# Places of the steps in the common order of all engines, set anew in every stage of a four-layer transformer kernel

## Chip, cores and metric

One core of a Trainium2 chip. The metric is the time of the device in microseconds (us), the median of several runs. The engines are named as in the profile: PE is TensorE (PEld its weight loads), DVE is VectorE, ACT is ScalarE, POOL is GpSimd and SP is SyncE, which here issues all DMAs.

## The reference

x has the shape (2, 1024, 256): two batches of 1024 tokens. Four layers run one after the other. Each has self-attention, cross-attention to a context of 77 tokens, and an MLP; each of the three parts is added to x and has a layer norm ahead of it whose scale and shift come from a conditioning vector. In short:

```python
for layer in (L0, L1, L2, L3):
    h = ada_ln(x, cond)                       # 16 heads
    q, k, v = heads(h @ Wq), heads(h @ Wk), heads(h @ Wv)
    x = x + softmax(q @ k.T * scale) @ v @ Wo + bo      # 1024 x 1024 scores a head
    h = ada_ln(x, cond)
    x = x + softmax(heads(h @ Wq2) @ heads(ctx @ Wk2).T * scale) @ heads(ctx @ Wv2) @ Wo2 + bo2
    h = ada_ln(x, cond)
    x = x + gelu(h @ W1 + b1) @ W2 + b2       # L3: a gated MLP of twice the width
```

Layers 0 and 1 have heads of width 16, layers 2 and 3 of width 64. Layer 2 also turns q and k by rotary position factors (rope), in both attentions. All of it is fp32.

## The kernel before

**Stages.** The work runs in stages: for each layer a self-attention, a cross-attention and an MLP stage. For layers 0 and 1 (narrow) self and cross are laid into one plan; for layers 2 and 3 (wide) each stage has its own. At the end of a plan all engines drain and wait for each other. In the profiled execution the stages lie about here: narrow self 75 to 575 us and 880 to 1375 us, narrow cross up to 745 and 1548, their MLPs behind them; layer 2: self 1697 to 2640, cross 2710 to 3003, MLP to 3175; layer 3: self 3175 to 4050, cross 4100 to 4385, MLP to 4535.

**Common order.** All engines walk one list of steps, `order`. A step such as ("cs", S, n, j) has a part for each engine that takes part in it: `tensor_program`, `scalar_program`, `vector_program`, `gpsimd_program` and `sync_program` each loop over the whole list and issue their own instructions of every step, with waits on semaphores for what the others must have done. So an engine never takes a step out of turn, and the order of the list is the order of every engine's queue. The list is made by `Plan`: `put` gives each step a place, a number counted in units of the stage (lo for one step, or spread evenly from lo to hi), and `close` sorts by place, with ties in order of entry.

**Units.** In a self stage a unit is a group of heads (4 narrow, 2 wide) times 512 queries, in 8 key tiles. Per tile and half: `score` (PE: K times Q into PSUM; ACT: exponential, L1469) and `av` (PE, L1194). Scores are shifted by each query's negated maximum, which the steps of the unit ahead make: `max` (PE scores the other way round, L1087 wide and L1091 narrow; DVE reduces, L1757 and L1761), narrow only `mjoin` (DVE joins two halves, in the tile NMX, L1776), `mturn` (PE transposes, L1151 or L1149; DVE copies, L1788; SP sends the row into the query tile by DMA, L2144). The output: `fin` (ACT copies, L1479), the sums of the exponentials, `norm`, `proj` (PE, L1236 wide and L1246 narrow; DVE adds to x, L1850 wide and L1854 narrow). Wide units sum the exponentials by `acc_p` (POOL, tiles 0 to 5, L2031 and L2035) and `acc_v` (DVE, tiles 6 and 7, L1814), then `sum` (PE, L1204) and `norm` in two halves (DVE: reciprocal L1829, product L1831). Narrow ones use `sums16` (PE L1213, DVE L1822), `spread16` (ACT, L1509) and `norm` (PE L1221, DVE L1838).

**Wide cross units** (32 a stage, 2 heads and 512 queries each): `cs` for each head (PE scores, L1015; DVE takes the maximum, L1797; ACT makes exponentials with their sums, L1490), `cnorm` (DVE: reciprocal, L1806; POOL: product, L2022), `cturn` (PE transposes, L1118; ACT copies, L1498), `cav` (PE, L1130), `fin` (ACT, L1479), `proj` (PE L1236, DVE L1850).

**Work beside the units.** `nat64`, `p16`, `val16` and `v64` make Q, K and V from the normed input (PE, with copies on ACT and differences on DVE, L1728 where there is no rope). With rope a chain follows each `nat64`: copy (ACT L1435), `rcos` (DVE L1742, POOL L2008), `rturn` (POOL L2015 and L2016), `rhigh` (ACT L1441), `rlow` (DVE L1749). `keep16`, `stack16`, `qstack` and `kstack` are DMAs on SP that lay Q and K out for the heads (stack16: L2127, 6 transfers a group in a cross stage). `w_load` and `w_split` bring weights, `m_load` (SP, L2278) and `m_split` (DVE L1929, POOL L2041) those of the MLP. `norm_put` places the layer norm of the next part: statistics, root, `ln_norm` (DVE L1649), `ln_turn` (PE L1036, ACT L1408), `ln_split` (DVE, up to L1662), `ln_bias`. In an MLP stage `up` (PE, ACT, DVE) and `down` (PE, L1324) alternate.

**PSUM.** The free banks are handed out in turn by `take`; a step that takes a bank waits until it was freed three takes before (wide self: two). `small` is another ring, of one bank, for `mturn` and `sum` in wide self stages.

The functions that set the places are `core64_steps` (L633), `core_steps` (L657), `kv64_steps` (L687) and the loop over the stages (L750 on). The two that decide what a unit looks like are short in their core:

```python
            for at, step in ((-1.25, ("cs", S, u.n, 0)), (-0.85, ("cs", S, u.n, 1)), (-0.45, ("cnorm", S, u.n)),
                             (0.2 * S.L.rope, ("cturn", S, u.n)), (0.5 + 0.2 * S.L.rope, ("cav", S, u.n)),
                             (0.51 + 0.2 * S.L.rope, ("fin", S, u.n)), (1.3 + 0.15 * S.L.rope, ("proj", S, u.n, 0))):
                plan.put(u.n + at, 0, [step])
```

## Time and profile before

| what | value |
|---|---|
| runs of the kernel before | 4522.99 us median of 3 (4517.64 to 4530.47) |
| profiled execution | 4537.6 us; its span, first to last instruction, 4535.8 us |
| mean granted clock of TensorE | 0.948 |
| PE, DVE, ACT, POOL busy | 90%, 66%, 46%, 30% of the span |
| DMA | 269.28 MB, mean 59 GB/s |

How to read it: a line such as "PE PS L1118 <- POOL t L2022: 33.7, 32, 3.5" says that PE, ahead of its instructions of line 1118, stood idle for 33.7 us in all, in 32 cases, at most 3.5 us, until GpSimd's instruction of line 2022 had ended. In a timeline the brackets hold the idle time ahead of an instruction and what ended it. The granted clock is 1 at 2.4 GHz and 0.5 at 1.2 GHz, so 0.948 is a mean over stretches at either.

### The profile page before, as it was taken

The numbers are of one execution on the slowest core, as the hardware profiler recorded it, in microseconds if no ns is written. First come the engines' busy times: TensorE is split into PE (matmuls) and PEld (weight loads), VectorE is DVE, ScalarE is ACT, GpSimd is POOL, SyncE is SP. The second block draws the span as 40 slices with busy tenths as digits, with TensorE's granted clock in tenths as the row PEclk, the third lists the DMA queues.
The fourth block names the chain that finished last, engine by engine and source line by source line (L and its number), as shares of the span: only waits on it lengthen the run. The fifth ranks groups of instructions, "written<-read, shape, count | busy, mean of one in ns | idle before, by whom it ended". The sixth has DMA issues, their size and how long they took to land.

```text
span 4535.8 us, 55477 instructions
## 1 busy us (share of the span) xinstructions
PE 4070.6 (90%) x20428; PEld 2486.0 (55%) x20428; DVE 3010.2 (66%) x4405; ACT 2076.4 (46%) x3756; POOL 1349.6 (30%) x664
## 2 busy tenths in 40 slices
PE   7999979799998888998999967888999999997889
PEld 5343357634335675555555545666555555546668
DVE  5888755688885666777777844345677777764355
ACT  2656645255564543443444435553444344435541
POOL 1100011100001035655555543321444444441120
PEclk8999989899998999999999978998999999998999
DMA  4223230312323142331333222323232222214220
GB/s 131 39 43 49 44 70 24 56 30 43 47 44 63 32 88 63 66 65 39 65 66 66 63 65 67 70 61 63 69 70 60 67 66 66 60 47 108 68 54 20
DMA packets 151983, 269.28 MB, mean 59 GB/s; under 512 B 34090, under 2 KB 67812, under 8 KB 150688
## 3 DMA queue, kind: packets, MB, share of 16 engines
q1 hardware_dynamic: 151712, 265.72, 27.9%
q8 instruction: 163, 2.67, 0.3%
q14 instruction: 108, 0.88, 0.1%
HBM read 105.01 MB, written 29.64 MB: 30 GB/s over the span
## 4 chain that ended last, share of the span: by engine, by line
PE 38%; DVE 8%; ACT 4%; POOL 4%; issue 4%; SPq 3%; DMA 1%; POOLq 0%; DVEq 0%; ACTq 0%
PE PS L1015 19%; PE PS L1194 7%; PE PS L1087 4%; PE PS L1236 4%; PE PS L1324 2%; DVE t L1757 2%; SPq L2173 2%; ACT t L1490 1%; DVE PS L1829 1%; SPq L2190 1%; POOL t L2035 1%; PE PS L1118 1%; POOL t L2022 1%; POOL t L2008 1%; PE PS L1204 1%
## 5 line engine op out<-in xcount | busy, mean ns | idle before, releaser
L1015 PE MATMUL PS<-t 128*128 128x512 f32 (+4 forms) x7896 | 1988.9, 384 | 160.4 <-ACT t L1469 24.8
L1469 ACT ACTIVATE t<-PS 128x512 f32<-128x512 f32 (+2 forms) x1600 | 1166.9, 750 | 1124.7 <-PE PS L1015 1118.3
L1015 PEld LDWEIGHTS PS<-t 128*128 128x128 f32 (+2 forms) x7896 | 1253.8, 188 | 708.9 <-issue 253.5
L1194 PE MATMUL PS<-t 128*32 128x512 f32 (+2 forms) x4352 | 809.7, 610 | 0.2
L1757 DVE TENSOR_REDUCE t<-PS 128x1 fp32r<-128x1024 f32 x512 | 622.0, 1220 | 281.4 <-PE PS L1087 275.8
L1761 DVE TENSOR_REDUCE t<-PS 128x1 f32<-128x512 f32 x1024 | 651.4, 684 | 73.1 <-PE PS L1091 70.7
L2035 POOL TENSOR_TENSOR t<-t 128x1024 f32<-128x1024 f32 x256 | 617.6, 2412 | 133.6 <-ACT t L1469 106.9
L1091 PE MATMUL PS<-t 96*128 96x512 bf16 x1024 | 370.3, 394 | 34.8 <-DVE t L1761 14.3
L1087 PE MATMUL PS<-t 128*128 128x512 f32 x1024 | 339.9, 415 | 58.8 <-DVE t L1757 36.4
L2031 POOL TENSOR_TENSOR t<-t 128x1024 f32<-128x1024 f32 x64 | 155.0, 2422 | 734.4 <-PE PS L1204 442.1
L1194 PEld LDWEIGHTS PS<-t 128*32 128x32 f32 (+2 forms) x4352 | 170.7, 122 | 329.1 <-issue 324.4
L1972 POOL TENSOR_TENSOR t<-t 128x2048 f32<-128x2048 f32 x24 | 112.0, 4668 | 788.1 <-DMA t<-in_rows 528.6
L1091 PEld LDWEIGHTS PS<-t 96*128 96x128 bf16 x1024 | 97.1, 98 | 358.2 <-DVE t L1761 135.4
L1236 PE MATMUL PS<-t 128*128 128x256 f32 x1024 | 260.3, 399 | 27.5 <-DVE t L1742 10.9
L1850 DVE TENSOR_TENSOR t<-PS,t 128x1024 f32<-128x1024 f32 x128 | 156.3, 1221 | 166.3 <-PE PS L1236 166.3
L1087 PEld LDWEIGHTS PS<-t 128*128 128x128 f32 x1024 | 195.5, 197 | 127.6 <-DVE t L1757 53.3
L1236 PEld LDWEIGHTS PS<-t 128*128 128x128 f32 x1024 | 197.7, 199 | 69.2 <-issue 23.9
L1829 DVE RECIPROCAL PS<-PS 128x256 f32<-128x256 f32 x128 | 224.7, 1755 | 11.8 <-PE PS L1204 11.8
L1324 PE MATMUL PS<-t 128*128 128x256 f32 x1536 | 219.0, 295 | 10.4 <-DVE t L1946 5.8
L1324 PEld LDWEIGHTS PS<-t 128*128 128x128 f32 x1536 | 207.6, 199 | 22.8 <-DVE t L1946 5.5
L1490 ACT ACTIVATE t<-PS,t 128x77 f32<-128x77 f32 x512 | 159.3, 325 | 132.3 <-DVE t L1797 132.1
L1946 DVE TENSOR_TENSOR t<-t 128x512 fp32r<-128x512 f32 x128 | 113.6, 888 | 138.8 <-ACT t L1572 137.5
(131 smaller groups left out, 3804.9 us busy)
## 6 DMA issues: line engine op xcount, KB each, us to landing
t<-t SPq DMA_DIRECT2D x640, 128.0 KB, 2.5
t<-scr_n SPq DMA_DIRECT2D x288, 128.0 KB, 6.4
t<-t SPq DMA_DIRECT2D x128, 256.0 KB, 3.8
scr_n<-t SPq DMA_DIRECT2D x72, 256.0 KB, 2.3
t<-t SPq DMA_DIRECT2D x256, 64.0 KB, 2.0
t<-in_L_Wg SPq DMA_DIRECT2D x16, 768.0 KB, 4.6
t<-in_L_W SPq DMA_DIRECT2D x36, 256.0 KB, 3.2
t<-in_L_Wo SPq DMA_DIRECT2D x64, 128.0 KB, 2.5
```

The costliest lines, as they stand in the source:

```text
L1015: ins = e.matmul(out, l, r, start=i == 0, stop=i == len(terms) - 1, tile_position=tp)
L1087: ins = e.matmul(o[:, 512 * h:512 * h + 512], u.smq[j][qt], u.smk[j][h], start=True, stop=True)
L1091: e.matmul(o, u.smq[j][qt], u.smk[j][half], start=True, stop=True).then_inc(*bank_full[k].inc(nth))
L1194: ins = e.matmul(banks[S.ot][wd * j:wd * j + wd, :], u.v[j][kt], P[0:S.pr, j, :], start=kt == 0, stop=kt == S.nkt - 1, tile_position=(0, w ...
L1236: ins = e.matmul(o[:, 256 * q:256 * q + 256], S.OR[n % 2][:, 128 * q:128 * q + 128], u.wo[:, :], start=True, stop=True)
L1324: ins = e.matmul(banks[4 + q][:, 0:D], l, r, start=m == 0 and t == 0, stop=m == 7 and t == 2)
L1469: e.activation(dst, src, ACT.Exp, scale=S.L.scale).then_inc(*expd.inc((S.i, i)))
L1490: ins = e.activation(S.PQ[n % 3][:, j, t, :], o[:, 256 * t + CT * b:256 * t + CT * b + CT], ACT.Exp, bias=S.NM[n % 3][:, at], accum_out=S. ...
L1757: e.tensor_reduce(S.MT[m % 2][:, S.nqt * j + qt:S.nqt * j + qt + 1], o, AX.X, ALU.max, negate=True).then_inc(*bank_free[k].nth(nth))
L1761: e.tensor_reduce(S.NMX[:, 4 * j + qt, half:half + 1], o, AX.X, ALU.max).then_inc(*bank_free[k].nth(nth))
L1829: e.reciprocal(o[:, hs], o[:, hs]).then_inc(*recip_made.inc((S.i, n, h)))
L2035: e.tensor_tensor(S.AP_[:, :, :], S.AP_[:, :, :], P[1][:, :, :], ALU.add).then_inc(*pool_summed.inc((S.i, n, kt)))
```

## The change

No step is added or removed. The numbers given to `put` change in every stage; so the common list, and with it the queue of every engine, has another order. Two places need more than a number. The narrow stages' NMX is held twice, by turns of the unit, because the first max steps of the next unit now stand ahead of the last transposition of this one; SBUF use stays as it was, by a smaller filler. And in layer 2 one group makes the second half of its queries ahead of the first, so the DMA that stacks them waits for both halves. The diff, cut to its core:

```diff
@@ attention_tiles
-            S.NMX = sbt(c, [128, 16, 2])
+            S.NMX = [sbt(c, [128, 16, 2]) for _ in range(2)]
@@ core64_steps
-            for at, step in ((-1.25, ("cs", S, u.n, 0)), (-0.85, ("cs", S, u.n, 1)), (-0.45, ("cnorm", S, u.n)),
-                             (0.2 * S.L.rope, ("cturn", S, u.n)), (0.5 + 0.2 * S.L.rope, ("cav", S, u.n)),
-                             (0.51 + 0.2 * S.L.rope, ("fin", S, u.n)), (1.3 + 0.15 * S.L.rope, ("proj", S, u.n, 0))):
+            places = ((-1.25, -0.774, -0.45, -0.038, 0.7, 0.71, 1.523) if S.L.rope else
+                      (-1.51, -1.07, -0.59, -0.071, 0.5, 0.56, 1.921))
+            for at, step in zip(places, (("cs", S, u.n, 0), ("cs", S, u.n, 1), ("cnorm", S, u.n), ("cturn", S, u.n),
+                                         ("cav", S, u.n), ("fin", S, u.n), ("proj", S, u.n, 0))):
...
-                    plan.put((i + 1.2) / k, 0, [("acc_p", S, n, kt)])
+                    plan.put((i + 0.489) / k, 0, [("acc_p", S, n, kt)])
...
-                    plan.put((i + 1.3) / k, 0, [("acc_v", S, n, kt)])
+                    plan.put((i + 0.859) / k, 0, [("acc_v", S, n, kt)])
...
-                    for at, step in ((2.76, ("sum", S, n)), (2.77, ("fin", S, n)), (4.2, ("norm", S, n, 0)),
-                                     (5.2, ("norm", S, n, 1)), (7.2, ("proj", S, n, 0))):
+                    for at, step in ((2.76, ("sum", S, n)), (2.77, ("fin", S, n)), (3.451, ("norm", S, n, 0)),
+                                     (4.2, ("norm", S, n, 1)), (7.2, ("proj", S, n, 0))):
@@ core_steps (sums16, spread16, norm, proj, proj)
-        tail = (0.2, 0.45, 0.7, 1.2, 1.45) if S.cross else (0.07, 0.25, 0.4, 0.53, 0.72)
+        tail = (0.2, 0.182, 0.7, 1.2, 1.45) if S.cross else (0.07, 0.082, 0.4, 0.53, 0.72)
@@ narrow cross
-                            at = (-3, 3.05)[b] + 0.8 * ch
+                            at = (-3, 3.132)[b] + 0.444 * ch
...
-                        plan.put((-1.95, -1.95, 0.05, 0.05, 4.5, 4.6, 6, 8)[g], 0, [("stack16", S, g)])
-                        plan.put((-1.2, -0.7)[g] if g < 2 else 2 * g - 2.2, (-0.7, -0.2)[g] if g < 2 else 2 * g - 0.7,
+                        plan.put((-1.95, -1.95, 0.05, 0.05, 4.5, 6.232, 6, 8.524)[g], 0, [("stack16", S, g)])
+                        plan.put((-1.306, -0.663)[g] if g < 2 else 2 * g - 1.981, (-0.7, 0.504)[g] if g < 2 else 2 * g - 0.7,
...
-                        plan.put(5 + 0.9 * j, 0, [("m_load", M, j)])
+                        plan.put(3.494 + 0.9 * j, 0, [("m_load", M, j)])
@@ narrow self
-                    plan.put(5.6, 7.6, [("val16", S, 1, t) for t in range(8)])
+                    plan.put(2.989, 7.245, [("val16", S, 1, t) for t in range(8)])
...
-                        plan.put(max(n - 1.3, 0), n - 0.3, max_steps(S, n))
+                        plan.put(max(n - 1.331, 0), n - 0.362, max_steps(S, n)[:-1])
+                        plan.put(n - 0.3, 0, max_steps(S, n)[-1:])
@@ wide cross (o = 4 * g - 9)
-                            nat64_chain(plan, S, g, 0, (o + 1.3, o + 2.9), (0, 0.15, 0.3, 0.95, 1.1))
+                            nat64_chain(plan, S, g, 0, (o + 1.647, o + 2.737), (0, 0.022, 0.3, 0.968, 1.081))
...
-                            plan.put(o + 2.3, o + 3.7, nat64_steps(S, g, 0))
+                            plan.put(o + 3.125, o + 3.7, nat64_steps(S, g, 0))
...
-                        plan.put(2 * pi - 4.5, 0, [("qstack", S, pi)])
+                        plan.put(2 * pi - 3.632, 0, [("qstack", S, pi)])
@@ wide self, rope (o = 4 * g - 4)
-                            plan.put(o + (0.1 if g != 4 else 0.45), o + (0.5 if g != 4 else 0.75),
+                            plan.put(o + (0.684 if g != 4 else 0.45), o + (0.5 if g != 4 else 1.194),
...
-                            for qk, at in ((1, (0.35 + late, 0.8 + late * 0.8)), (0, (1.25 + late * 0.5, 1.65 + late * 0.2))):
+                            for qk, at in ((1, (0.35, 0.81)), (0, (1.234, 1.65))) if g != 4 else (
+                                    (1, (0.65, 1.04)), (0, (2.114, 1.613))):
@@ wide self, no rope (v64, nat64 of K, nat64 of Q)
-                        for at, to, steps in zip((0.1, 0.55, 1.2) if g != 4 else (0.55, 1.0, 1.5),
-                                                 (0.5, 1.1, 1.9) if g != 4 else (0.95, 1.45, 1.95),
+                        for at, to, steps in zip((0.226, 0.856, 1.776) if g != 4 else (0.561, 1, 1.212),
+                                                 (0.5, -0.232, 1.9) if g != 4 else (0.95, 1.408, 1.988),
@@ MLP (layer norm of the next stage: first place, gap of the statistics, pace)
-                plan.put(max(2 * (i % 4) - 2.5, -2) if way == "up" else 2 * i + 0.2, 0, [("m_split", S, j)])
+                plan.put(max(2 * (i % 4) - 2.5, -2) if way == "up" else 2 * i + -0.122, 0, [("m_split", S, j)])
...
-                        plan.put(at + m + 2.5, 0, [("down", S, b, half, m)])
+                        plan.put(at + m + 2.696, 0, [("down", S, b, half, m)])
...
-                    at, gap, pace = (17.65, 0.05, 1.2) if b else (0.9, 0.35, 2)
+                    at, gap, pace = (17.808, 0.05, 0.913) if b else (0.9, 0.714, 2)
@@ vector_program
+                if m >= 2:
+                    w.wait_ge(max_part, (S.i, m - 2))
                 o, k, nth = full(w, ("max", S.i, m, j, qt, half))
-                e.tensor_reduce(S.NMX[:, 4 * j + qt, half:half + 1], o, AX.X, ALU.max).then_inc(*bank_free[k].nth(nth))
+                e.tensor_reduce(S.NMX[m % 2][:, 4 * j + qt, half:half + 1], o, AX.X, ALU.max).then_inc(*bank_free[k].nth(nth))
```

The rest of the diff moves further steps by less (places of the layer norms, of the key and value work of layers 2 and 3, of the first group's nat64 in the MLP stages).

## Rows read from the trace of the kernel before

**Rows 1.** The page: its head line and part 1 (busy time of each engine).

```profile
span 4535.8 us, 55477 instructions
PE 4070.6 (90%) x20428; PEld 2486.0 (55%) x20428; DVE 3010.2 (66%) x4405; ACT 2076.4 (46%) x3756; POOL 1349.6 (30%) x664
```

**Rows 2.** Busy time by stretch; columns in the first line, x counts instructions, PEclk mean granted clock.

```profile
core 0: us, PE busy (x) PEld busy (x) DVE busy (x) ACT busy (x) POOL busy (x), PEclk, DMA share, GB/s
...
1697.00:2640.00 943.00, 871.09 (x3666) 503.68 (x3666) 699.68 (x652) 395.70 (x634) 545.07 (x247) 0.97 0.28 60
2710.00:3003.00 293.00, 243.34 (x1276) 182.50 (x1275) 126.29 (x227) 163.35 (x589) 106.31 (x70) 0.91 0.27 62
3175.00:4050.00 875.00, 836.14 (x3604) 489.04 (x3605) 626.72 (x610) 366.11 (x600) 386.15 (x160) 0.99 0.28 64
4100.00:4385.00 285.00, 239.66 (x1304) 183.00 (x1304) 121.30 (x222) 156.67 (x594) 50.17 (x35) 0.94 0.31 72
```

**Rows 3.** Waits of PE in 4100:4385, layer 3's cross stage (total us, times, longest).

```profile
PE PS L1118 <- POOL t L2022: 33.7, 32, 3.5
```

**Rows 4.** Timeline of one unit of layer 3's cross stage (start us, duration us).

```profile
4255.45 1.23 DVE L1850 TENSOR_TENSOR t<-PS,t 128x1024 f32<-128x1024 f32 x1 [1.25 <-PE PS L1236]
...
4256.60 0.19 DVE L1806 RECIPROCAL t<-t 128x8 f32<-128x8 f32 x1
...
4256.87 1.22 POOL L2022 TENSOR_TENSOR t<-t 128x616 f32<-128x616 f32 x1 [5.29 <-DVE t L1806]
...
4258.14 1.10 PE L1118 MATMUL PS<-t 128*77 128x128 f32 x8 [0.56 <-POOL t L2022]
```

**Rows 5.** Waits of PE in 2710:3003, layer 2's cross stage.

```profile
PE PS L1130 <- ACT t L1498: 21.7, 13, 3.9
PE PS L1118 <- POOL t L2022: 12.0, 9, 6.6
PE PS L1236 <- ACT t L1490: 4.3, 10, 1.2
PE PS L1236 <- DVE t L1742: 4.2, 6, 1.0
```

**Rows 6.** Groups by line in 2710:3003: GpSimd's rope work (busy us, mean ns).

```profile
L2008 POOL TENSOR_TENSOR t<-t 128x1024 f32<-128x1024 f32 x12 | 28.3, 2359 | 74.6 <-ACT t L1435 57.2 <-issue 17.4
...
L2016 POOL TENSOR_TENSOR t<-t 128x512 f32<-128x512 f32 x12 | 15.2, 1269 | 0.0
```

**Rows 7.** Timelines of SP and PE in layer 0's cross stage; waits of PE in 1375:1548.

```profile
638.98 5.54 SPq L2127 DMA_DIRECT2D t<-scr_n  x12
...
645.33 0.55 SPq L2144 DMA_DIRECT2D t<-t  x1
...
656.98 1.07 PE L1015 MATMUL PS<-t 97*77 97x512 bf16 x2 [7.53 <-DMA t<-t]
...
PE PS L1015 <- DMA t<-t: 4.5, 1, 4.5
```

**Rows 8.** Waits of PE in 1697:2640, layer 2's self stage.

```profile
PE PS L1087 <- DVE t L1757: 18.7, 12, 5.2
...
PE PS L1204 <- DVE t L1814: 10.0, 8, 1.8
...
PE PS L1151 <- DVE t L1831: 2.7, 3, 1.5
```

**Rows 9.** Waits of PE in 880:1375, layer 1's self stage.

```profile
PE PS L1149 <- DVE t L1776: 4.0, 3, 2.3
```

**Rows 10.** The instructions of L1509 (spread16) in 75:575.

```profile
L1509 ACT ACTIVATE t<-t x15: 618/631/632, 151.4 to 569.7; 128x512 f32<-128x512 f32 x15
```

**Rows 11.** Waits of PE in 745:880, the end of layer 0's MLP.

```profile
PE PS L1015 <- DVE t L1662: 6.6, 1, 6.6
```

**Rows 12.** L1814 (acc_v) and L1749 (rlow) in 1697:2640: duration ns min/median/max.

```profile
L1814 DVE TENSOR_TENSOR t<-t x62: 1206/1218/3473, 1757.3 to 2626.4; 128x1024 f32<-128x1024 f32 x62
...
L1749 DVE TENSOR_TENSOR t<-t x28: 1207/1604/3409, 1750.1 to 2508.6; 128x1024 fp32r<-128x1024 f32 x28
```

54 lines of the change are left out of this document (27 added, 27 removed).

## Prediction

> **What bounds the kernel now.** I read the page first, then the busy time by stage, then in each attention stage what TensorE (PE) waited for, and last the timeline where one wait came back every unit. The page shows a PE kernel: 4070.6 us busy of a span of 4535.8 [rows 1]. No step is added or removed, so PE's own work stays as it is, and the change can only move the 465 us in which PE stood still and the time that a low clock added.
>
> By stage [rows 2] the self-attention of layers 2 and 3 is PE at 92% and 96% (871.09 of 943, 836.14 of 875), while the two wide cross-attention stages stand at 83% and 84% (243.34 of 293, 239.66 of 285), with a granted clock of 0.91 and 0.94 against 0.97 and 0.99. Per microsecond the cross stages have the most to give. In layer 3's, PE waits for GpSimd's cnorm multiply 32 times, once in every unit, 33.7 us in all [rows 3], 1.05 us each. The timeline of one unit says why [rows 4]: VectorE adds the projection (4255.45, 1.23 us), only then takes cnorm's reciprocal (4256.60), GpSimd multiplies (4256.87, 1.22 us), and PE starts cturn the moment that ends, after 0.56 us idle. The reciprocal was not late for want of data; it stood behind the add, which stood behind PE's projection. In layer 2's cross stage the same engine waits otherwise [rows 5]: 21.7 us for ScalarE's cturn copy ahead of cav, 12.0 for GpSimd, and 4.3 and 4.2 ahead of the projection, 42.2 in these four.
>
> **The change, part by part.** A place matters only where it puts a step past another step on the same engine. The orders below follow from the numbers of the diff, sorted for one engine at a time.
>
> (a) Cross, layer 3. PE's cycle was cturn(n), cs1(n+1), proj(n-1), cav(n), cs0(n+2); it becomes cs0(n+2), cav(n), proj(n-1), cturn(n+1), cs1(n+2). On VectorE cnorm(n+1) (place 0.41) now comes ahead of the projection's add (0.921) instead of behind it (0.55 against 0.30). After cs1, PE has cs0, cav and proj before it needs cnorm's result, as before, but the add no longer delays the reciprocal. In the rows the add's 1.23 us lay ahead of the reciprocal, and a stall is 1.05 us on average [rows 3, 4], so removing it covers the stall. I take 26 of the 33.7 us, since next in line is ScalarE (cturn's copy now stands ahead of cs1's exponentials). Ends: -34 and 0.
>
> (b) Cross, layer 2. PE's cycle becomes cturn(n+1), cs1(n+2), proj(n), cav(n+1), cs0(n+3): exactly layer 3's old one. ScalarE's cturn copy is then ahead of cs1's exponentials, so the 21.7 us go. But cnorm (0.55) is still behind the add (0.523), so layer 3's stall comes with the order: 32 times 1.05, 33.7 us. GpSimd also has rope work here, 12 chains of 2.36 (rcos) + 2 x 1.27 (rturn's two operations, taken alike) = 4.9 us [rows 6]. Before, the sine multiply of every first half stood just ahead of a cnorm (2.45 against 2.55); now it stands just behind one (2.67), so I add only 2 us. 36 against 42.2: -6. Ends: -42, if nothing takes their place, and 33.7 + 12 x 4.9 - 42.2 = +50, if every chain delays a cnorm.
>
> (c) Cross, layers 0 and 1. PE stands 7.53 us in layer 0 and 4.5 in layer 1 for a row of negated maxima [rows 7]. SP issued it at 645.33, right behind the 12 transfers of stack16 for groups 4 and 5 (issued from 638.98), and PE went on at 656.98, 11.65 us later. Now stack16 of group 5 moves from place 4.6 to 6.232, behind this row (5.16), while a weight load of twice a transfer's size comes ahead of it: 8 parts of 12 are left, so the row lands 3.9 us earlier, in both layers: -8. Ends: -12 and 0. Here SP's queue is the thing moved past: m_load goes 1.5 places earlier and waits for the split three chunks before; what is queued behind is the next row's transfer, due most of a unit later, which covers it.
>
> (d) Self, layers 2 and 3. VectorE's adds acc_v of key tiles 6 and 7 go from 1.3 to 0.859 tiles behind their score and so ahead of one row-max reduce each; the two normalising steps go ahead by 0.75 and 1 tile, also ahead of a reduce each; GpSimd's acc_p goes ahead of rope work. PE's waits for acc_v (10.0) and for the normalised bank (2.7) in layer 2 [rows 8] should go: I take 10 of 12.7 and nothing in layer 3. The move of v64 and nat64 within their group I cost at nothing: PE's scores cover it, and if that cover is gone its price is of the size of the wait for reduces, 18.7 us [rows 8]. Ends: -30 and +20.
>
> (e) Self, layers 0 and 1. The join of the maxima now comes two max steps ahead of its transposition (NMX is doubled so that the next unit may start), which hides the 4.0 us wait of a layer [rows 9]. spread16 goes ahead of one exponential on ScalarE; it takes 0.631 us [rows 10], and ScalarE is idle near it. I take -3. Ends: -8 and 0.631 x 32 = +20.
>
> (f) MLP. The last layer-norm split of the next stage comes 0.85 place earlier, which should halve PE's 6.6 us wait for it [rows 11]: -4. Ends: -7 and 0, as the rest of the moves there pass nothing PE waits for.
>
> (g) Clock. Wide cross stands at 0.94 and 0.91 [rows 2]: between the levels of 1.2 and 2.4 GHz that is 12% of 285 and 18% of 293 us at the lower, 34 and 53 us, which cost 17 and 26. With fewer stalls I take 7 of these 43; ends -24 and 0. In the Trainium skill, "TensorE: Matmul & The Clock Gate" (section on HAM oscillation) ties the fall of the clock to long pauses, not to short ones like these; by that rule (g) is 0 and the sum 57.
>
> Sum: -(26 + 6 + 8 + 10 + 3 + 4 + 7) = -64 us against the profiled execution of 4537.6, thus 4473.6. That execution lies 14.6 above the median of the runs, 4523.0, so on their scale the forecast is 4459, 1.4% faster. About 0.3%, 14 us, is what a measurement of this kernel can tell from no change.
>
> **The rivals.** *More comes free* (chance 0.23): (a) in full, (b) with only half of layer 3's stall (-23), (c) -12, (d) -25, (g) -24: about 4400. For it: the freed stalls lie in stages whose clock is low. Against it: PE's weight loads have waits of their own that no order mends.
>
> *The gains cancel* (0.13): layer 2's cross stage takes over the stall that layer 3's loses, and the rope work adds to it, so that (b) is +40 against (a) -26, and (c) to (g) give only 20: 4517. For it: the order is the one whose row shows a wait in every unit. The changes might also do little of what their size suggests, since many places move without passing any step of an engine; I count that here.
>
> *VectorE's adds block the reduces* (0.09), the slower one. Place: wide self-attention, 124 acc_v in two layers, each of 1.22 us [rows 12], now ahead of a reduce whose bank PE's max matmul needs. If half passed through, 62 x 1.22 = 76 us, and (d) were lost: 4459 + 10 + 76 = 4545. It decides once a reduce ends later than PE reaches the second max behind it; PE waited for reduces 12 times in layer 2 [rows 8], 18.7 us, so the margin is mostly there. One acc_v lasted 3473 ns instead of 1218, and the median of rlow in layer 2's self stage is 1604 against a minimum of 1207 [rows 12]: a VectorE operation with two operands in SBUF is sometimes held up by something on GpSimd's side. The Trainium skill, "SBUF — State Buffer" (section Who interferes with whom), states just that: such an operation and a GpSimd operation that reads SBUF lock each other out entirely. By that rule more adds meeting more rope work would lengthen them.
>
> **How the numbers follow.** The forecast has 0.55. Faster by over 0.3% is it and the first rival, 0.78; the same 0.13; slower 0.09. The range: down to 4400, which leaves out some 0.06 of the first rival, and up to 4520, which takes in most of the cancelling case and leaves out 0.05 of it and the slower one. (b)'s upper end alone, +56 on the forecast, gives 4515, inside it.
>
> **What would show it.** (a) right: PE's wait for cnorm in layer 3's cross falls below 10 us and the stage shortens by 25 to 30. (b) right: the wait for the cturn copy is gone, the wait for cnorm is some 35 us. (c) right: the two waits for the row fall to about 3.6 and 0.6. (d) right: no wait for acc_v left in layer 2. (g) right: a clock of 0.95 or more in wide cross. The forecast is wrong if the wide self stages change by more than 20 us either way, or if layer 3's cross keeps its wait.

## The result, and the profile after

The changed kernel takes **4366.42 us** (median of 4 runs, 4359.09 to 4369.63), the kernel before on the same chip 4526.73 (4517.64 to 4535.87): ratio 0.9645, 95% interval 0.9633 to 0.9658. It is faster by 160 us, where 64 were forecast; the time lies below the range (4400). The sign was right, the size was wrong by a factor of 2.5.

The page of the changed kernel, its head, first part and two rows of the second (to hold against [rows 1]):

```profile
span 4367.9 us, 55496 instructions
...
PE 3992.2 (91%) x20428; PEld 2446.8 (56%) x20428; DVE 3020.0 (69%) x4405; ACT 2075.6 (48%) x3756; POOL 1368.1 (31%) x664
...
PE   7999989799998988998899977988999999998989
...
PEclk7999999999998998999999988999999999998999
```

The span is 167.9 us shorter. PE's instructions are the same 20428, but their busy time fell from 4070.6 to 3992.2, by 78.4, while the mean granted clock rose from 0.948 to 0.960; the time in which PE stood still fell by 89.5. So nearly half of the gain is PE doing the same work faster. An estimate from the two mean clocks puts 61 us of the 78.4 down to the clock (0.052 of 4535.8 less 0.040 of 4367.9, as if PE always had work); what the rest is, no run shows.

To see where it lies, I cut both executions at the first or last PE instruction of the same lines. "Untouched" is the range of the stage over those of my runs below that left its steps where they were, the profiled execution of before included; it is the ruler for every stage time that follows. The kernels e3 to e7, e9 to e11, e13, e14, e16 and e17 ran once each, so each of their stage times is one reading.

| stage (us) | untouched | after | change to the profiled before |
|---|---|---|---|
| layer 0: self, cross, MLP | 480.2 to 485.1, 189.0 to 192.3, 113.8 to 115.4 | 477.3, 178.7, 106.1 | -3.9, -12.9, -7.9 |
| layer 1: self, cross, MLP | 491.1 to 498.0, 188.6 to 190.5, 145.3 to 148.6 | 487.6, 180.5, 140.6 | -10.4, -8.9, -7.3 |
| layer 2: self, cross | 950.1 to 952.8, 293.2 (one) | 930.2, 256.4 | -19.9, -36.8 |
| layer 3: self, cross | 908.0 to 909.4, 266.3 to 272.8 | 889.0, 235.8 | -20.3, -37.0 |
| all the rest | 480.7 to 488.3 | 485.7 | -2.6 |

Ten of these executions have layer 3's cross stage untouched, and they tell what the spread is made of: PE's idle time there is 37.0 to 38.3 us in all ten, its busy time 228.2 to 234.7, at a clock of 0.96 to 0.94. So between single runs the idle time is the sharper measure, and a clock that differs by 0.02 tells nothing.

The same view as [rows 2], busy time by stretch, of the kernel after: layer 2's self and cross stage, layer 3's self and cross stage.

```profile
core 0: us, PE busy (x) PEld busy (x) DVE busy (x) ACT busy (x) POOL busy (x), PEclk, DMA share, GB/s
1647.50:2577.70 930.20, 868.50 (x3696) 505.41 (x3696) 697.77 (x655) 397.48 (x639) 559.22 (x248) 0.97 0.28 61
2633.80:2890.20 256.40, 226.44 (x1284) 172.53 (x1285) 130.45 (x230) 164.01 (x599) 112.64 (x70) 0.98 0.32 75
3045.50:3934.50 889.00, 854.12 (x3698) 500.84 (x3696) 645.13 (x628) 374.69 (x611) 395.24 (x164) 0.98 0.28 64
3970.90:4206.70 235.80, 223.30 (x1284) 176.57 (x1284) 125.35 (x218) 153.29 (x586) 48.64 (x34) 0.96 0.35 82
```

The clock of the cross stages went from 0.91 and 0.94 to 0.98 and 0.96; the second step is inside the spread of untouched runs. PE's idle time went from 48.9 to 30.0 us in layer 2's cross stage and from 38.2 to 12.5 in layer 3's. What PE waited for (total us, times, longest) in layer 3's cross stage (against [rows 3]), in layer 2's (against [rows 5]) and in layer 2's self stage (against [rows 8]):

```profile
PE PS L1120 <- POOL t L2026: 6.8, 4, 3.5
PE PS L1038 <- DVE t L1651: 5.6, 3, 3.6
```

```profile
PE PS L1120 <- POOL t L2026: 26.5, 20, 8.4
PE PS L1038 <- DVE t L1651: 4.5, 2, 4.3
PE PS L1017 <- DVE t L1744: 4.1, 5, 0.8
```

```profile
PE PS L1089 <- DVE t L1759: 21.7, 17, 5.1
PE PS L1089 <- DMA t<-t: 18.6, 8, 12.0
PE PS L1017 <- ACT t L1471: 6.5, 21, 0.4
```

L1120 and L2026 are cturn and cnorm's product, here two and four lines further down. In layer 3 the stall of every unit is gone. In layer 2 the wait for the cturn copy (21.7) is gone and cnorm's came, but at 26.5. The 8.4 us in it stand ahead of the stage's first cturn, so they belong to the hand-over before the stage; inside the stage it is 18.1 us in 19 times, against 12.0 in 9 before. In layer 2's self stage the waits for acc_v and for the bank are gone, and there is something new: 18.6 us for DMAs (3.7 before), 12.0 of them at once.

### The profile page after: what moved, and what is told of

Its sections match the earlier page's. It is cut to its first block, busy times and chain, and to the rows that moved or that the text cites. A ratio compares the mean times of both kernels' runs of the same rounds, so it can differ in the third digit from the quotient of the medians.

```text
span 4367.9 us, 55496 instructions
## 1 busy us (share of the span) xinstructions
PE 3992.2 (91%) x20428; PEld 2446.8 (56%) x20428; DVE 3020.0 (69%) x4405; ACT 2075.6 (48%) x3756; POOL 1368.1 (31%) x664
## 4 chain that ended last, share of the span: by engine, by line
PE 69%; DVE 14%; issue 4%; SPq 4%; ACT 3%; POOL 2%; DMA 2%; DVEq 0%; POOLq 0%; ACTq 0%
PE PS L1017 30%; PE PS L1196 13%; PE PS L1238 5%; PE PS L1093 4%; PE PS L1089 4%; PE PS L1326 3%; DVE t L1765 3%; PE PS L1248 3%; SPq L2178 2%; DVE t L1759 2%; SPq L2195 1%; PE PS L1223 1%; PE PS L1215 1%; PE PS L1120 1%; DVE PS L1833 1%
## 5 line engine op out<-in xcount | busy, mean ns | idle before, releaser
L1017 PE MATMUL PS<-t 128*128 128x512 f32 (+4 forms) x7896 | 1964.0, 380 | 118.9 <-DVE t L1674 16.5
L1017 PEld LDWEIGHTS PS<-t 128*128 128x128 f32 (+2 forms) x7896 | 1236.8, 185 | 632.8 <-issue 238.3
L1089 PEld LDWEIGHTS PS<-t 128*128 128x128 f32 x1024 | 194.4, 196 | 143.9 <-DVE t L1759 56.0
L1238 PE MATMUL PS<-t 128*128 128x256 f32 x1024 | 253.9, 392 | 15.5 <-DVE t L1835 9.1
L1833 DVE RECIPROCAL PS<-PS 128x256 f32<-128x256 f32 x128 | 224.7, 1756 | 13.6 <-PE PS L1206 13.6
L1238 PEld LDWEIGHTS PS<-t 128*128 128x128 f32 x1024 | 193.6, 195 | 72.4 <-issue 30.3
L1326 PE MATMUL PS<-t 128*128 128x256 f32 x1536 | 215.0, 291 | 9.1 <-POOL t L2045 5.5
L1326 PEld LDWEIGHTS PS<-t 128*128 128x128 f32 x1536 | 202.9, 195 | 21.5 <-POOL t L2045 5.9
L2026 POOL TENSOR_TENSOR t<-t 128x616 f32<-128x616 f32 x64 | 84.0, 1312 | 349.5 <-DVE t L1810 349.5
```

The lines of the kernel that those rows point to most:

```text
L1017: ins = e.matmul(out, l, r, start=i == 0, stop=i == len(terms) - 1, tile_position=tp)
L1089: ins = e.matmul(o[:, 512 * h:512 * h + 512], u.smq[j][qt], u.smk[j][h], start=True, stop=True)
L1238: ins = e.matmul(o[:, 256 * q:256 * q + 256], S.OR[n % 2][:, 128 * q:128 * q + 128], u.wo[:, :], start=True, stop=True)
L1326: ins = e.matmul(banks[4 + q][:, 0:D], l, r, start=m == 0 and t == 0, stop=m == 7 and t == 2)
L1833: e.reciprocal(o[:, hs], o[:, hs]).then_inc(*recip_made.inc((S.i, n, h)))
```

## The experiments

### Units or side work

My theory: the gain comes from the order inside the units (a, b, d), the side work's places cost and give nothing. The rival: it comes from the side work. The first kernel is the kernel before with the new places of the units alone, and of what lies outside them only stack16's; the second is its complement.

```diff
 # e1: before, with
+            places = ((-1.25, -0.774, -0.45, -0.038, 0.7, 0.71, 1.523) if S.L.rope else
+                      (-1.51, -1.07, -0.59, -0.071, 0.5, 0.56, 1.921))
...
+ acc_p 0.489, acc_v 0.859, norm 3.451 and 4.2, stack16 of group 5 at 6.232
 # e2: after, with exactly these as before
```

> The kernel before with only the unit orders of the wide stages new (seven places of a cross unit; acc_p, acc_v and norm of a self unit) and stack16 of group 5 behind the row of maxima. Theory U (the order inside a unit makes the gain, and fewer pauses give clock back): the whole change shortened layer 3's cross by 37.0 us, layer 2's by 36.8, the wide self stages by 19.9 and 20.3, the narrow cross stages by 12.9 and 8.9; here layer 3's cross -33 to -37, layer 2's -20 to -37, wide self -12 to -20 each, narrow cross -4 each; in all -85 to -115 us. Theory S (the side work's places, nat64, qstack, rope chain, make it): cross -26 and -6, wide self under -10 each, in all -50 us.

> The changed kernel with the unit orders of the wide stages and the place of stack16 of group 5 as before: what the other moves bring alone. If the two halves add up, this and the first run give 160 us together: theory U 45 to 75 us less than before, nearly all in layers 0 and 1 and their MLPs; theory S about 110, with 30 of it in layer 2's cross stage.

Measured: e1 4483.37 us, ratio 0.9887 (0.9864 to 0.9910); e2 4424.12, ratio 0.9766 (0.9748 to 0.9784). The side work alone gives twice what the units give. By stage, e1 against e2: layer 3's cross 237.0 against 271.7, so this one is the units' and nothing else's. Layer 2's cross 275.3 against 259.5, after 256.4: the units alone give 17.9 us of 36.8, the side work alone 33.7, so they do not add up. Layer 2's self **960.9** against 931.1 and layer 3's 912.2 against 892.4: here the units' new order costs 10.8 and 2.9 us when alone, and the side work gives 19.0 and 16.9. Narrow cross, stack16's move alone: 183.3 from 191.6 and 183.3 from 189.4.

### Single moves and single undos

```diff
 # e3: before, with one move a stage
+ L3 cross: cnorm -0.8 | L2 cross: cturn 0.1 | L2 self: acc_v 0.859 | L3 self: norm 3.451, 4.2
+ L0 self: join two steps ahead, NMX doubled | L1 self: spread16 0.082 | MLP 0, 1, 3: 17.808, 0.05, 0.913
 # e4: after, with one undo a stage
+ L3 cross: cnorm -0.075 | L2 cross: rope chain as before | L2, L3 self: v64 and nat64 as before
+ L0 self: val16 as before | L1 self: join as before
```

> The kernel before with one move in each stage, read stage by stage. Layer 3 cross: only cnorm ahead of the projection's add (place -0.8 for -0.45): if the reciprocal behind the add was the stall, -26 to -37 us with nothing else moved; if it was ScalarE's order, -5. Layer 2 cross: only cturn ahead of the second cs (0.1 for 0.2): -20 or more if ScalarE's cturn copy was its stall; about -6 by my prediction. Layer 2 self: only acc_v earlier: -8 by its 10.0 us wait. Layer 3 self: only the two norms earlier: 0 to -3. Layer 0 self: only join and transposition of the maxima apart: -3. Layer 1 self: only spread16 earlier: 0, up to +10 if ScalarE is blocked. MLPs of layers 0 and 1: only the layer norm's pace: -4 to -7 each.

> The changed kernel with one move undone in each stage, read stage by stage. Layer 3 cross: cnorm back behind the projection's add, in the new cycle: +30 or more if that place is what matters; under +10 if the new cycle has slack. Layer 2 cross: the rope chain's old places: +5 to +15 if keeping rope work off the front of cnorm matters, 0 if not. Layers 2 and 3 self: v64 and nat64 at their old places: 0 by my prediction (cost at nothing), +10 each by theory S. Layer 0 self: val16 at its old places, join and transposition together: +4 or less. Layer 1 self: join and transposition together again: +3.

Measured: e3 4488.54 us, e4 4557.89. **Layer 3's cross:** with cnorm alone ahead of the add 244.7, within 9 us of after's 235.8. Its wait falls from 33.7 to 9.6 us, while PE now waits for exponentials ahead of the projection (0.3 before):

```profile
PE PS L1122 <- POOL t L2028: 9.6, 8, 3.4
PE PS L1240 <- ACT t L1494: 8.7, 12, 4.9
```

With after's cycle and cnorm behind the add 357.4: PE waits 92.1 us for it and its clock falls to 0.84.

```profile
PE PS L1123 <- POOL t L2029: 92.1, 32, 7.1
```

So (a) is shown by e3, where cnorm passes only the add. e4 shows how much hangs on the place, but not on the add alone: there cnorm also falls behind the maximum of cs0 (0.49) and stands right ahead of cturn. **Layer 2's self:** acc_v's move alone 960.6, 10.5 us more, about what e1 lost (7.8 beyond the untouched range): the mechanism of my slower rival is real, at a quarter of its price for one layer (38 us), and it vanishes with the new side work (e2 931.1, after 930.2). The wait for the maxima's reduce grows from the 18.7 us of [rows 8] to

```profile
PE PS L1091 <- DVE t L1761: 32.6, 21, 4.6
```

Undoing v64 and nat64 costs 24.3 and 22.1 us in the two wide self stages, undoing the rope chain 17.1 in layer 2's cross. Layer 0's MLP: the layer norm's pace alone gives 106.1, just after's value; layer 1's 146.1, nothing. The join and spread16 alone: 480.5 and 493.3, nothing either; val16 and the join undone: 478.1 and 489.1, nothing. cturn's swap alone in layer 2's cross: 280.2, 13.0 less.

### Which side step

```diff
 # e5: L2 cross: rope chain; L2 self: v64; L3 self: nat64; L1 MLP: rope chain of the next group
+ nat64_chain(plan, S, g, 0, (o + 1.647, o + 2.737), (0, 0.022, 0.3, 0.968, 1.081))
+ plan.put(o + (0.684 if g != 4 else 0.45), o + (0.5 if g != 4 else 1.194), v64 ...
 # e6: wide cross: qstack; L2 self: nat64 chains; L3 self: v64
+ plan.put(2 * pi - 3.632, 0, [("qstack", S, pi)])
+ (1, (0.35, 0.81)), (0, (1.234, 1.65)); g == 4: (1, (0.65, 1.04)), (0, (2.114, 1.613))
```

> The kernel before with four single groups of side steps at their new places, one in each of four stages: layer 2's cross only the rope chain of the next group (nat64 1.647/2.737; 0, .022, .3, .968, 1.081); layer 2's self only v64 (0.684; 1.194 in group 4); layer 3's self only the two nat64 groups (v64 old); layer 1's MLP only the rope chain of the next stage's first group. The whole of the new places less the order of the units was worth 19.0 us in layer 2's self (from 950.1) and 16.9 in layer 3's (from 909.3). Theory A, the gain sits in the steps that PE itself computes and that feed the next group (v64 in layer 2, nat64 in layer 3): layer 2's self 935 or less, layer 3's self 897 or less. Theory B, it sits in the other half: layer 2's self above 945, layer 3's above 904. Layer 2's cross: if the rope chain's places carry the 33.7 us of the side work there, the stage falls from 293.2 to 265 or less; if weight and qstack places carry it, it stays above 280. Layer 1's MLP: its rope chain alone, if it is what shortened the stage by the 7 us that the layer-norm pace did not give, 147.9 to 142 or less; else 146 or more.

> The kernel before with the complementary halves: both wide cross stages only qstack (2 pi - 3.632 for 2 pi - 4.5); layer 2's self only the nat64 chains of Q and K (and qstack waiting for both halves); layer 3's self only v64 (0.226, 0.561 in group 4). Theory A (the gain of the wide self stages sits in v64 for layer 2 and nat64 for layer 3): layer 2's self above 945, layer 3's above 904. Theory B: 935 or less and 897 or less. If it is neither half alone but their order against each other, both runs stay within 6 us of the stage before. Layer 2's cross: if qstack's place carries part of the 33.7 us, below 285; if the rope chain's does, 291 to 296, and layer 3's cross, whose side work brought nothing beyond cnorm, 270 to 275.

Measured: e5 4461.68 us, e6 4506.26. Layer 2's cross: the rope chain alone 258.6, qstack 288.7. Layer 2's self: v64 alone 930.1, **all of the gain**; the nat64 chains 950.9, with one new wait of 9.0 us for a DMA in it, so the rest of the stage got shorter by about as much. Layer 3's self: nat64 -6.6, v64 -9.7. Layer 1's MLP: nothing.

### One step of the rope chain

Eight kernels cut the chain's move in layer 2's cross stage down. The same kernels try v64 at other places in layer 2's self stage, and single moves elsewhere.

```diff
 # e7:  L2 cross: rcos of each first half at +0.26, behind cnorm
 # e9:  L2 cross: first half from o+1.647.  L2 self: v64 at .25, .35.  L3 self: K.
 #      L1 MLP: K and V projections.  Narrow cross: m_load.  Narrow self: val16
 # e10: L2 cross: second half from o+2.737.  L3 self: Q.  MLP 0, 1: down 2.696.
 #      Narrow cross: row maxima.  L1 self: join two steps ahead
 # e11: L2 cross: both halves, old distances.  MLP 0, 1: statistics 0.714 apart.
 #      Narrow cross: projections' copies, layer norm
 # e13: L2 cross: second half from o+2.76.  L2 self: v64 at .592, .684
 # e14: L2 cross: second half's projection alone at o+2.737.  L2 self: v64 at .38, .44
 # e16: L2 cross: rhigh of the second half alone, o+3.71.  L2 self: v64 at .47, .53
 # e17: L2 cross: second half from o+2.76, rhigh and rlow stay.  L2 self: v64 at .70, .75
```

> The kernel before with one step moved, in layer 2's cross stage only: GpSimd's sine multiply (rcos) of each rope chain's first half at +0.26 instead of +0.15, so from just ahead of a unit's cnorm to just behind it; 6 instructions of some 2.4 us. Theory A, the long GpSimd multiply ahead of cnorm is what held PE up in this stage: 6 times up to 2.4 us and what follows from it, the stage falls from 293.2 to 283 or less. Theory B, it is the rest of the chain (PE's turns and VectorE's reads of them) or the other side steps: 290 or more. All other stages within 2 us of before.

> The kernel before with, in each stage, one thing: (1) layer 2's cross: only the first half of the next group's rope chain starts at o+1.647 instead of o+1.3 (its five steps at their old distances), so PE projects it behind the projection of unit n-1 instead of between cturn and it, and GpSimd multiplies behind cnorm and not ahead of it. The two chains with all new distances were worth 34.6 us (293.2 to 258.6). If the first half carries it: 270 or less; if the second half or the distances do: 283 or more. (2) Layer 2's self: v64 of the next group at o+0.25 and o+0.35 instead of o+0.1 and o+0.3, thus just behind the last use of the buffer that ScalarE copies it into (PE's last product of the unit before stands at o+0.22). Theory A, the 20 us of v64 came from ScalarE standing before that buffer with its exponentials queued behind: 938 or less. Theory B, it came from v64's place beside the row maxima and the rope chain: 945 or more. (3) Layer 3's self: only K's two nat64 steps; K and Q together gave 6.6 us: 903 to 905 if it is K, 909 if Q. (4) Layer 1's MLP: only the K and V projections' places (1.588 and 1.713 apart): 141 to 143 if these are what shortened the stage by 7.3, else 146 to 148. (5) Cross of layers 0 and 1: only the MLP's weight loads at 3.494; the stages lost 8.0 and 3.3 us without stack16's move: 184 and 186 if these loads carry it, within 1.5 of 191.6 and 189.4 if not. (6) Self of layers 0 and 1: only val16's places: 1 to 4 us less in each, or nothing.

> The kernel before with: (1) layer 2's cross: only the second half of the rope chain starts at o+2.737 instead of o+2.9, so ahead of the next unit's scores: 270 or less if the second half carries the 34.6 us, 283 or more if not. (2) Layer 2's self unchanged: 948 to 952, a control. (3) Layer 3's self: only Q's two nat64 steps: 903 to 905 if Q carries the 6.6 us, 909 if K. (4) MLPs of layers 0 and 1: only down at 2.696 instead of 2.5 (PE's second product a fifth of a chunk later): if it is what shortened layer 1's, 141 to 143; layer 0's 114 to 108; else within 1.5 us of 114.0 and 147.9. (5) Cross of layers 0 and 1: only the places of the row maxima: 184 and 186 if they carry the rest of the gain, within 1.5 us if not. (6) Self of layer 1: the maxima's join two steps ahead of its transposition, with the doubled buffer; the wait ahead of the transposition was 4.0 us: 494 or less from 498.0; layer 0's stays within 2 us of 481.2.

> The kernel before with: (1) layer 2's cross: both halves of the rope chain start at their new places (o+1.647, o+2.737), but its five steps keep their old distances (0, .15, .3, .95, 1.1). If the starts carry the 34.6 us: 265 or less; if the distances do (GpSimd's multiply .022 behind the projection and not .15, VectorE's subtraction 1.081 and not 1.1): 280 or more. (2) MLPs of layers 0 and 1: only the first part's layer-norm statistics spaced .714 and not .35: 141 to 143 and 106 to 108 if these shortened the stages, else within 1.5 us of 147.9 and 114.0. (3) Cross of layers 0 and 1: only the copies of the next part's projections (3.132, .444 apart, for 3.05, .8 apart) and the layer norm ending at 3.054: 184 and 186 if they carry the rest, within 1.5 us if not. (4) All other stages within 2 us of before.

> The kernel before with: (1) layer 2's cross: the second half of the rope chain starts at o+2.76 instead of o+2.9, so 0.14 earlier, but still behind the next unit's first scores (o+2.75). Theory A, what counts is that PE does this projection ahead of those scores: the stage stays at 287 or more. Theory B, what counts is that the chain runs earlier: 272 or less. (2) Layer 2's self: v64 at o+0.592 and o+0.684 like the kernel after, but its two halves in their natural order. If the place between K's two rope projections carries the 20.0 us: 934 or less; if the swapped order does: 945 or more.

> The kernel before with: (1) layer 2's cross: only the projection itself (and ScalarE's copy of it) of the second half starts at o+2.737, the four rope steps behind it stay where they are (o+3.05 to o+4.0). Theory A, PE's projection ahead of the next unit's scores is what counts: 272 or less. Theory B, the earlier chain: 283 or more. (2) Layer 2's self: v64 at o+0.38 and o+0.44, right behind the projection of K's first half (o+0.35) and ahead of GpSimd's multiply and turn of it (o+0.40, o+0.45) in the order, so that PE has two products to do while GpSimd turns K. If the point is that work stands between the rope projection and the copy that waits for the turn (o+0.65): 936 or less; if the later place beside the row maxima is what counts: 944 or more.

> The kernel before with: (1) layer 2's cross: one step moved, ScalarE's copy of the turned second half (rhigh) at o+3.71 instead of o+3.85, which puts it ahead of the next unit's first exponentials (o+3.75) and not behind them. Theory A: the copy stood behind eight exponentials, VectorE's subtraction stood behind the copy, the next row maxima behind that, and so the exponentials and the copy of cturn that PE waits for; the copy's move alone carries the gain: 275 or less. Theory B: the whole chain has to run earlier: 285 or more. (2) Layer 2's self: v64 at o+0.47 and o+0.53, behind VectorE's and GpSimd's reads of K's projected first half (o+0.40, o+0.45) and ahead of the copy that waits for the turn (o+0.65). If v64's products are to stand between the turn and its copy, with the banks free: 936 or less; if they have to stand yet later: 944 or more.

> The kernel before with: (1) layer 2's cross: the second half's projection, multiply and turn 0.14 earlier (o+2.76, 2.91, 3.06), rhigh and VectorE's subtraction where they were (o+3.85, o+4.0). Theory A (the copy behind the exponentials is the cause): 285 or more. Theory B (the earlier chain): 275 or less. (2) Layer 2's self: v64 at o+0.7 and o+0.75, behind the copy and the subtraction of K's first half (o+0.65, o+0.69) and ahead of the projection of its second half (o+0.8). If v64 is to fill the time of GpSimd's turn: 944 or more; if it is only to stand clear of the first half's chain: 936 or less.

Measured (us; before 293.2, with PE idle for 48.9, and 950.1; the whole chain's move in e5 258.6, idle 29.1):

| kernel | time | layer 2's cross | PE idle in it | layer 2's self |
|---|---|---|---|---|
| e7 | 4524.88 | 290.0 | 50.4 | 952.8, untouched |
| e9 | 4505.03 | 285.1 | 45.1 | 947.4 |
| e10 | 4484.46 | 264.6 | 34.3 | 951.7, untouched |
| e11 | 4476.92 | 259.9 | 30.6 | 952.3, untouched |
| e13 | 4480.74 | 268.4 | 37.2 | 929.6 |
| e14 | 4530.12 | 288.1 | 46.0 | 963.7 |
| e16 | 4494.08 | **269.9** | 36.5 | 941.5 |
| e17 | 4501.22 | **291.3** | 49.2 | 931.3 |

**Layer 2's cross.** The second half carries it (e10), not PE's order (e13 keeps it and gains, e14 changes it and gains 5 us). Of its steps it is one: ScalarE's copy `rhigh`, 0.14 of a unit earlier, gives 23.3 us by itself (e16), 12.4 of them idle time; the three steps ahead of it, moved without `rhigh` and `rlow`, give 1.9 and leave the idle time as it was (e17). That is most of the 19.8 us of idle time that the whole chain's move takes away; the rest came with the larger moves of e10 and e11. The timeline of before, ScalarE's accumulator reads left out, shows what it did (start us, us, engine, line; in brackets the idle time before it):

```profile
2858.45 1.22 POOL L2022 TENSOR_TENSOR t<-t 128x616 f32<-128x616 f32 x1
2858.51 0.60 ACT L1479 ACTIVATE t<-PS 128x512 f32<-128x512 f32 x1 [1.18 <-PE PS L1130]
...
2860.19 0.33 ACT L1490 ACTIVATE t<-PS,t 128x77 f32<-128x77 f32 x1 [1.08 <-DVE t L1797]
...
2861.40 1.06 ACT L1441 ACTIVATE t<-t 128x1024 fp32r<-128x1024 f32 x1
...
2862.50 1.23 DVE L1749 TENSOR_TENSOR t<-t 128x1024 fp32r<-128x1024 f32 x1 [2.35 <-ACT t L1441]
2863.64 0.47 DVE L1797 TENSOR_REDUCE t<-PS 128x4 f32<-128x308 f32 x1
...
2864.15 0.33 ACT L1490 ACTIVATE t<-PS,t 128x77 f32<-128x77 f32 x1 [1.68 <-DVE t L1797]
...
2865.37 1.02 ACT L1498 ACTIVATE t<-PS 77x1024 f32<-77x1024 f32 x1
...
2866.44 1.12 PE L1130 MATMUL PS<-t 77*64 77x512 f32 x2 [2.80 <-ACT t L1498]
```

ScalarE copies (L1441) only behind the exponentials of the first head. VectorE stands 2.35 us before the subtraction (L1749), and the maximum of the second head (L1797), whose scores may long be there, stands behind it. ScalarE waits 1.68 for that maximum, then has four exponentials ahead of the cturn copy, and PE waits 2.80. This wait stands five times in the stage, 2.80 us each, and once with 3.86. The same place in e16, where the lines are three further down:

```profile
2835.19 1.05 ACT L1444 ACTIVATE t<-t 128x1024 fp32r<-128x1024 f32 x1
2835.85 0.48 DVE L1800 TENSOR_REDUCE t<-PS 128x4 f32<-128x308 f32 x1 [1.43 <-PE PS L1018]
2836.27 1.23 DVE L1752 TENSOR_TENSOR t<-t 128x1024 fp32r<-128x1024 f32 x1
...
2837.42 0.47 DVE L1800 TENSOR_REDUCE t<-PS 128x4 f32<-128x308 f32 x1
...
2837.92 0.33 ACT L1493 ACTIVATE t<-PS,t 128x77 f32<-128x77 f32 x1 [0.22 <-DVE t L1800]
...
2840.20 1.08 PE L1133 MATMUL PS<-t 77*64 77x512 f32 x4 [0.39 <-ACT t L1501]
```

From `fin`'s copy (L1479, here L1482 at 2834.70) to PE's product it is 5.50 us in place of 7.93. The copy waited for nothing but its place: GpSimd, which does the turn ahead of cnorm, had begun cnorm's product at 2858.45. The stage's PE, in the windows of e16 and e17:

```profile
2690.10:2960.00 269.90, 233.36 (x1275) 174.92 (x1276) 125.85 (x230) 164.13 (x599) 106.33 (x70) 0.94 0.30 71
```

```profile
2680.80:2972.10 291.30, 242.08 (x1275) 183.28 (x1276) 126.24 (x230) 164.22 (x599) 106.34 (x70) 0.91 0.28 66
```

12.7 of the 21.4 us between them are idle time, 8.7 are PE's busy time; of such a difference in busy time up to 6.5 us stood between runs of one order in layer 3's cross stage.

**Layer 2's self, v64.** At .25/.35 it gives 2.7 us, at .38/.44 it costs 13.6, at .47/.53 it gives 8.6, at .592/.684 20.5, at .70/.75 18.8. Two theories fall. The buffer: e9 puts v64 behind the last use of the buffer that ScalarE copies it into, and ScalarE's wait ahead of that copy for PE's product (27.7 us in 5 times) is gone, yet 17 of the 20 us are not. The filler: e14 puts the two products where GpSimd turns K, and PE now waits for K's banks instead (total us, times, longest):

```profile
PE PS L1018 <- DVE t L1745: 20.8, 5, 4.6
```

while e17, behind the whole chain of K's first half, is as good as e13. What would fit all five is that v64 must not stand next to K's first projection (o+0.35): the two take banks from one ring, and the next row maxima would then find none. PE's wait for a maxima's reduce ahead of a projection (L1015 for L1757) is 6.5 us in before, 8.0 in e9, 9.3 in e14 and under 1 in e5, e13 and e17; e16 has none either, but waits 9.0 for K's banks. That is a reading of the waits, and it is not shown: I did not try a larger ring. In e5 the wait is gone, one for exponentials falls from 12.2 to 7.1 us, and the two make up the idle time that the stage loses (72.1 to 60.2; the other 8.1 us are busy time). But the changed kernel, with v64 clear of the projection too, has 4.5 us of this wait and e12 has 5.3, and both have the gain. In layer 3, where K's projection stands at o+0.55, v64 just behind its buffer did give 9.7 us (e6), with the same 27.7 us of ScalarE gone.

**The others.** Layer 3's self: K alone 909.3, Q alone 903.5 (of 909.3). Layer 1's MLP: K and V projections 142.5, statistics 143.6, down 146.6, of 147.9. Cross of layers 0 and 1: MLP loads 188.0 and 190.0, row maxima 190.7 and 188.6, copies and norm **185.3 and 186.1**. Layer 1's self 494.0 (val16) and 490.8 (join), inside or at the edge of the untouched range.

### Two tries at a faster kernel

```diff
 # e8: after, with
-            places = ((-1.25, -0.774, -0.45, -0.038, ...
+            places = ((-1.25, -0.774, -0.6, -0.038, ...
+ w_load of group 1 at -19.9 instead of -9 (wide cross)
 # e12: after, with
-                                    (1, (0.65, 1.04)), (0, (2.114, 1.613))):
+                                    (1, (0.65, 1.04)), (0, (1.4, 1.71))):
```

> The kernel after with cnorm in layer 2's cross stage at -0.6 instead of -0.45, which puts it ahead of the projection's add as in layer 3's, and the weight load of group 1 of both wide cross stages issued at -19.9, ahead of kv_stack, instead of -9. In the kernel after, PE waits 26.5 us for GpSimd's cnorm multiply in this stage (20 times) and 13.0 us for that weight split in the hand-over before it. Theory A, cnorm is late for the same reason as in layer 3's cross stage before (the reciprocal stands behind the add): the stage falls from 256.4 to 238 or less, the hand-over from 56.1 to 50 or less; the time is 4330 to 4350 against 4366. Theory B, it is late because GpSimd has the rope chain to do: the stage stays within 6 us of 256.4 and the wait for cnorm stays above 15 us; then the time is 4355 or more, by the weight load alone.

> The kernel after with one thing undone: in layer 2's self stage Q's rope chain of group 4 at (1.4, 1.71) as before, instead of (2.114, 1.613). In the kernel after, PE stands 12.0 us once for a DMA ahead of the row maxima of unit 16 (9.0 us in the run that has only the new chain places), 15.9 units into the stage; at 2.114 the first half of Q's chain stands at place 14.1, behind the place 14.05 of the transfer of unit 16's queries, which waits for it. Theory A, that chain is late and costs what the wait shows: layer 2's self falls from 930.2 to 920 or less, the time from 4366 to 4351 to 4358. Theory B, the late chain keeps other work out of the way and its wait comes back in another place: the stage 926 or more, the time 4362 or more.

e8: 4359.68 us, ratio 0.9631 (0.9615 to 0.9647), not to be told from after's 0.9645. The wait for cnorm did fall, inside the stage from 18.1 to 7.0 (with the first one, ahead of the stage, from 26.5 to 15.4), and the stage still grew from 256.4 to 262.9:

```profile
2630.00:2893.00 263.00, 233.66 (x1285) 178.60 (x1284) 133.28 (x228) 162.76 (x597) 107.93 (x70) 0.93 0.31 72
```

Idle time is 29.3 us, after's 30.0, since PE now waits for exponentials ahead of the projection (1.9 in after), as in e3:

```profile
PE PS L1239 <- ACT t L1493: 8.9, 18, 4.9
```

PE's busy time is 7.1 us more, at a clock of 0.93 against 0.98. Theory A missed. Theory B came close with its numbers (the stage is 6.5 us off, where it had 6, the wait 15.4 with the first one), but its reason fails: most of the wait did go with the place ahead of the add. The weight load did not touch the 13.0 us wait in the hand-over, which is VectorE's, not the transfer's.

e12: **4353.24 us**, ratio 0.9624 (0.9603 to 0.9644), the lowest median of all. Its own ratio's interval overlaps after's; what shows the gain is the stage, 915.7 against 930.2 in after and 926.0 in e8, which has after's places there (10.3 to 14.5 us), and the row that is gone. In after, and in e12 all waits of PE for a DMA in that stage:

```profile
2113.26 1.22 PE L1089 MATMUL PS<-t 128*128 128x512 f32 x2 [11.96 <-DMA t<-t]
```

```profile
PE PS L1089 <- DMA t<-t: 6.8, 8, 1.7
```

The change had put the first half of Q's chain of group 4 behind the place of the transfer that waits for it. It is a loss of some 12 us inside a change that won 20 there.

## Why the prediction was wrong

The forecast missed 104 us of the 168 between the two profiled executions. Two thirds of the miss, 71 us, are PE's busy time, for which (g) had 7; 33 us are idle time, 89.5 where (a) to (f) had 57. Three steps failed: (g) was sized far too small, (d) set the move of v64 and nat64 at nothing, and (b) set the rope work at 2 us.

**(a), right.** Forecast -26, measured -37.0 (-30.5 against the untouched range's lower end). The wait fell from 33.7 to 6.8 us, 26.9, just what I took; the rest is PE's busy time, 234.6 to 223.3, which I had put into (g) as 7 us for both stages.

**(b), right for the units, wrong for the side work.** I forecast -6 from an exchange of stalls; it was -36.8, of it 17.9 busy time and 18.9 idle. The exchange took place: e1, the units' order alone, lost the 21.7 us wait and waited 31.7 in the stage for cnorm, near the 33.7 + 2 that I had worked out, and its idle time fell by 6.3. What failed is the sentence that set the rope work at 2 us: with the side work the idle time falls by 12.6 more and the wait for cnorm is 18.1. I followed the chain only on GpSimd, past cnorm, and in e7 this passing takes away no idle time (50.4 against 48.9). I did not sort ScalarE's queue by the new places, where `rhigh` passes the first exponentials; that one step gives 23.3 in the kernel before, 12.4 of it idle time.

**(c), right, undersized.** Both waits for the row are gone (1.0 us and none left of 12.0), where I had 8 us; stack16 alone gives 8.3 and 6.1 (5.7 and 5.3 beyond the untouched ranges). The copies of the projections, not costed, give 3.7 and 2.5 beyond these ranges (e11); the two stages together gave 21.8.

**(d), the mechanism that failed worst.** "The move of v64 and nat64 within their group I cost at nothing": in layer 2 v64's alone gives 20.0 us, the whole of the stage's gain, in layer 3 v64 gives 9.7 and nat64 6.6 of 20.3. The two stages gave 40.2 where I had 10, at the very line of 20 us each beyond which I had called the forecast wrong. The wait for acc_v did go, but acc_v's move, from which I took 10, costs 10.5 when alone. The total has the right sign by luck. Why v64's place is worth so much stays open.

**(e) and (f).** Self of layers 0 and 1: -3 forecast; at most 3 and 3.5 us lie beyond the untouched ranges, and no single move gave them. MLP: 4 forecast, 15.2 measured. The wait for the last split did go, and its pace gives all 7.9 us in layer 0. In layer 1 it gives nothing; there it is the K and V projections (5.4) and the statistics (4.3; against the untouched range's lower end 2.8 and 1.7).

**(g), the term that was sized worst.** 7 forecast for the wide cross stages, up to 24 as its bound, and nothing for the others; PE's busy time fell by 78.4, of it 29.2 in the wide cross stages, 17.9 in the wide self stages and 31.4 elsewhere. By the rule that I cited from the Trainium skill, "TensorE: Matmul & The Clock Gate" (HAM oscillation), that long pauses bring the clock down, this term was to be 0. In layer 3's cross stage before, the 32 waits for cnorm averaged 1.05 us, beside one of 5.8 for something else. With less of them PE's busy time, 228.2 to 234.7 us in the untouched runs, fell to 222.3 in e3, at a clock of 0.99, and rose to 267.7 at 0.84 in e4, where they were longer. The same page has a second case, in its section "A second HAM failure mode: psum-queue depth-cycling": frequent short idle times between groups of matmuls, with which the clock oscillates too. The runs here go that way: e3 still has one wait of 4.9 us and the highest clock. How short or how many the pauses must be, no run separates.

Of the rivals, *more comes free* was nearest and stopped at 4400: it had 24 us for the clock and nothing for the side work. *VectorE's adds block the reduces* shows at 10.5 us in e3, and is covered in the changed kernel.

## What to carry to other kernels

When places in a hand-written order move, sort every engine's queue by the old and by the new places and read where a step passes another, for the helpers' small copies too: a copy that is needed much later can hold the maxima, the exponentials and at last TensorE. The cross stages here paid for their many short pauses twice, once idle and once in busy time at a lower clock, so a sum over waits alone came out too small. Compare idle times before stage times when each kernel ran once. And look through a change that won for the part that lost: here one pair of its numbers cost some 12 us.

## What was not expected of the hardware

The same idle time does not mean the same clock: e8's layer 2 cross stage has 29.3 us idle at 0.93, after's 30.0 at 0.98. Nor does the same order: the untouched runs of layer 3's cross stage, with 37.0 to 38.3 us idle, stand at 0.94 to 0.96, with busy times up to 6.5 us apart. So e8's 7.1 us need not come from its order; what sets the clock from one execution to the next was not found.

VectorE's `rlow`, a subtraction with both operands in SBUF, took 2140 ns on average in layer 2's self stage before and 1517 after, for 28 instructions each, and 1512 in e6, which has only the new chain places:

```profile
L1749 DVE TENSOR_TENSOR t<-t 128x1024 fp32r<-128x1024 f32 x28 | 59.9, 2140 | 3.5 <-ACT t L1441 3.5
```

```profile
L1751 DVE TENSOR_TENSOR t<-t 128x1024 fp32r<-128x1024 f32 x28 | 42.5, 1517 | 3.1 <-ACT t L1443 3.1
```

It is 17.4 us shorter in the sum because it meets GpSimd less: these 28 had GpSimd's operations beside them for 41.7 us before and 23.3 after, and the 8 in either run with none beside them took at most 1227 ns. The rule of "SBUF — State Buffer" in the Trainium skill (Who interferes with whom) says that such an operation contends with a GpSimd operation that reads SBUF; the trace agrees. What this is worth to the stage is not shown: e6's was 950.9 against 950.1, with a new DMA wait of 9.0 us in it.
